# Second attention of a ViT block: scores as one float32 product, biases of q and k added on GpSimd, a PSUM bank written for each use, new step lists

## The reference, cut to what matters

```python
h = tok(x)                                   # (128, 197, 192)
h = h + attn(_layernorm(h), Wq, bq, ...)     # first attention, 12 heads of 16
# second attention, x = _layernorm(h)
qkv = (x @ qkv_w + qkv_b).reshape(B, N, 3, H, HD)
q, k, v = ...                                # HD = 64, H = 12
q = _layernorm(q, q_norm_w, q_norm_b)        # over the 64 of a head, times w, plus b
k = _layernorm(k, k_norm_w, k_norm_b)
attn = softmax(einsum('bhqd,bhkd->bhqk', q * scale, k))
o = einsum('bhqk,bhkd->bhqd', attn, v)
o = masked_gates[..., None] * o              # gates from softmax and top-2 of 10
h = h + (o.reshape(B, N, H * HD) @ proj_w + proj_b)
```

## Time and profile before

| | |
|---|---|
| median of 3 runs | 6208.34 us |
| time of the profiled execution | 6208.79 us |
| its span, first to last instruction | 6207.0 us |
| PE busy (share of the span) | 5808.5 us (94%) |
| PEld | 4640.1 us (75%) |
| DVE | 5098.7 us (82%) |
| ACT | 4936.7 us (80%) |
| POOL | 2435.5 us (39%) |
| transfers | 17 GB/s, 5.6% of the 16 DMA engines |
| granted clock of TensorE, mean | 0.993 |

### The profile page before, as it was taken

The page is one execution under the profiler, slowest core; times in us unless marked ns, Lnnn a source line. Parts: engine busy times, 40 slices in busy tenths (PEclk is TensorE's granted clock), DMA queues, the critical chain, the costliest instruction groups (busy, mean ns, idle before and its releaser), DMA issues.

```text
span 6207.0 us, 204792 instructions
## 1 busy us (share of the span) xinstructions
PE 5808.5 (94%) x63792; PEld 4640.1 (75%) x63792; DVE 5098.7 (82%) x16573; ACT 4936.7 (80%) x18945; POOL 2435.5 (39%) x2438
## 2 busy tenths in 40 slices
PE   3899999999999999999999999999999999999998
PEld 3677777777777777777777777777777777777776
DVE  4788888888888888888888888888888888888886
ACT  1788887887888888788888878888887887888886
POOL 0333443343344344334334433433433343444343
PEclk8999999999999999999999999999999999999999
DMA  1000000000000000000000000000000000000000
GB/s 64 16 19 16 15 19 16 15 15 19 16 15 19 16 15 15 19 16 15 19 16 15 17 17 16 15 19 16 15 19 16 15 15 19 16 15 19 16 15 5
DMA packets 60493, 106.58 MB, mean 17 GB/s; under 512 B 8077, under 2 KB 33945, under 8 KB 60129
## 3 DMA queue, kind: packets, MB, share of 16 engines
q1 hardware_dynamic: 60456, 106.12, 5.6%
HBM read 86.72 MB, written 19.37 MB: 17 GB/s over the span
## 4 chain that ended last, share of the span: by engine, by line
PE 60%; DVE 27%; issue 8%; ACT 4%; DVEq 1%; SPq 0%; ACTq 0%; POOL 0%; DMA 0%; POOLq 0%
PE bank L500 54%; PE bank L684 6%; DVE nmax L1034 5%; DVE qkn L1028 4%; DVE qk L916 3%; ACT p L745 3%; DVE kl L1018 2%; DVE ql L1012 2%; DVE v L996 2%; DVE nmax L921 2%; DVE gn L1044 1%; DVE x1T L911 1%; DVE rsum L1041 1%; DVE rsum L929 0%; DVE glog L963 0%
## 5 line engine op out<-in xcount | busy, mean ns | idle before, releaser
L489 POOL TENSOR_TENSOR pq<-pq,gn 99x788 f32<-99x788 f32 x768 | 1166.3, 1519 | 2302.6 <-DVE gn L1044 2302.4
L792 ACT ACTIVATE pq<-bank,nmax 99x197 f32<-99x197 f32 x3072 | 1303.1, 444 | 300.5 <-DVE nmax L1034 300.5
L745 ACT ACTIVATE p<-bank,nmax 99x197 f32<-99x197 f32 x3072 | 1281.9, 441 | 31.2 <-DVE nmax L921 15.1
L921 DVE TENSOR_REDUCE nmax<-bank 99x2 f32<-99x394 f32 x1536 | 824.4, 565 | 320.8 <-PE bank L500 316.8
L1034 DVE TENSOR_REDUCE nmax<-bank 99x2 f32<-99x394 f32 x1536 | 837.9, 559 | 125.3 <-PE bank L500 110.1
L798 ACT ACTIVATE pT<-bank 99x394 f32<-99x394 f32 x1536 | 773.1, 512 | 152.7 <-PE bank L684 152.3
L684 PE MATMUL bank<-ident,pq 99*99 99x99 f32 (+1 forms) x6144 | 784.7, 260 | 14.8 <-ACT pq L792 3.3
L500 PE MATMUL bank<-x2T,wqkc 128*128 128x198 f16 (+1 forms) x7680 | 796.3, 249 | 1.0 <-ACT qkc L756 0.6
L684 PEld LDWEIGHTS bank<-ident,pq 99*99 99x99 f32 (+1 forms) x6144 | 647.5, 166 | 171.1 <-issue 78.4
L500 PEld LDWEIGHTS bank<-x2T,wqkc 128*128 128x128 f16 (+1 forms) x7680 | 650.0, 98 | 99.1 <-ACT qkc L756 41.4
L792 ACT ACTIVATION_READ_ACCUMULATOR pq<-bank,nmax 99x1 f32 x3072 | 687.9, 224 | 0.0
(11 more groups left out here) (149 smaller groups left out, 11877.8 us busy)
## 6 DMA issues: line engine op xcount, KB each, us to landing
xa<-in_xa SPq DMA_DIRECT2D x128, 300.1 KB
xb<-in_xb SPq DMA_DIRECT2D x128, 300.1 KB
out_tokens<-res SPq DMA_DIRECT2D x128, 74.2 KB
out_tokens<-res SPq DMA_DIRECT2D x128, 73.5 KB
p<-in_wq SPq DMA_DIRECT2D x1, 1152.0 KB
pT<-in_wk SPq DMA_DIRECT2D x1, 1152.0 KB
qkc<-in_basis SPq DMA_DIRECT2D x1, 661.5 KB
sq<-in_wq SPq DMA_DIRECT2D x1, 576.0 KB
```

What stands on the lines that cost most here:

```text
L489: nc.gpsimd.tensor_tensor(pair, pair, factor, op=ALU.mult).then_inc(s_sc.up(), 1)
L745: last = nc.scalar.activation(p1[0:TC, h, c, :], psum("s1", h)[0:TC, c * T:c * T + T], ACT.Exp, bias=nmax1[:, c, h:h + 1], accum_out=sum1[ ...
L792: last = nc.scalar.activation(pq[0:TC, h % SLOTS, c, 0:T], psum("s2", h)[0:TC, c * T:c * T + T], ACT.Exp, bias=nmax2[:, h, c:c + 1], accum ...
L921: V.tensor_reduce(nmax1[:, :, h], psum("s1", h)[0:TC, 0:2 * T].rearrange("p (a b) -> p a b", a=2), op=ALU.max, axis=AX.X, negate=True).the ...
```

## The change

Tiles `qh`, `ql`, `kh`, `kl` and the steps that write them (ACT `rstd` and `kh`, DVE `lo` and `kl`) go. A new POOL step `bias` adds `ln_b` to both q and k of a pair in one instruction on 128 x 396 elements, from `qkn` into a new float32 tile `qkb`. Step `s2` waits for it (`s_qk`) and makes the scores by float32 matmuls straight from `qkb`: 4 a pair instead of 12, still on two halves of the array's rows and in two banks. DVE's `rstd` waits for the bias of three pairs earlier in place of `kl` and `lo` (the ring of `qkn`). Banks are no longer rings: each use in PE's list names its bank (`@15`: head n in bank 1, head n + 1 in bank 5). All four lists are new. Four more iterations are straight code instead of the loop (`LEAD`), two at each end. The helper `lasts`, which found the last reader of each bank, is replaced by a wait for the last head of a group, and bank `ms` is counted as number 0.

```diff
 
 
 
-BANKS = {"tok": (2,), "x1T": (2,), "qk1": (0, 1), "v1": (2,), "s1": (0, 1), "ctx": (2,), "wo": (2,),
-         "x2T": (6,), "gl": (6,), "qk": (6,), "v2": (6,), "ms": (7,),
-         "rstd": (3, 4, 5), "s2": (3, 4, 5), "pT": (3, 4, 5), "o2": (3, 4, 5), "proj": (3, 4, 5)}
-
 ORDER = {
     "pe": """
-3:tok 0:pT_9 0:pT_10 0:o2_3 0:pT_11 1:rstd1 0:o2_4 0:o2_5 1:s2_0 0:proj 1:v2_1 3:x1T 1:rstd2 1:s2_2 1:v2_2 1:rstd3
-3:qk1_0 1:v2_3 3:v1 3:s1_0 2:x2T 1:rstd4 1:s2_4 3:qk1_1 2:qk0 1:rstd5 1:pT_0 3:s1_2 2:gl 1:s2_6 1:pT_1 3:qk1_2 2:qk1
-1:pT_2 3:s1_4 3:ctx0 2:qk2 1:pT_3 1:s2_8 2:qk3 3:s1_6 2:ms0 2:qk4 1:o2_0 1:o2_1 3:s1_8 1:pT_4 1:pT_5 2:qk5 2:ms1
-3:s1_10 3:ctx1 1:s2_10 1:o2_2 2:ms2 2:v2_0 3:ctx2 1:pT_6 3:wo 1:pT_7 1:pT_8 2:rstd0
+3:tok@2 0:pT_8@0 0:pT_9@7 0:pT_10@4 0:pT_11@5 1:rstd2@3 0:o2_2@6 0:o2_3@1 0:o2_4@6 0:o2_5@4 1:s2_0@15 1:s2_2@64
+3:x1T@0 0:proj@2 3:qk1_0@5 1:v2_0@7 3:qk1_1@2 3:s1_0@04 3:s1_2@63 1:v2_1@5 1:v2_2@1 3:qk1_2@7 1:s2_4@50 1:rstd3@2
+1:pT_0@4 1:v2_3@1 2:x2T@3 1:pT_1@6 3:s1_4@57 1:s2_6@24 2:qk0@6 3:v1@3 2:qk1@0 1:rstd4@1 1:rstd5@2 2:qk2@6 3:s1_6@51
+3:s1_8@34 2:qk3@0 1:pT_2@6 2:gl@2 2:qk4@7 2:qk5@5 1:pT_3@2 1:s2_8@03 3:s1_10@75 1:pT_4@6 3:ctx0@1 1:o2_0@4 1:s2_10@72
+2:ms0@0 2:ms1 2:ms2 3:ctx1@5 3:ctx2@6 1:o2_1@3 1:pT_5@4 1:pT_6@5 3:wo@1 1:pT_7@7 2:rstd0@4 2:rstd1@3
 """,
     "dve": """
-3:fold 1:v2_0 1:var2 0:gr5 2:wo 1:rstd0 1:gate3 3:tok 1:kl0 1:rstd1 1:lo0 2:nx2 1:s2_0 3:nx1 1:lo1 1:s2_1 0:proj 1:kl1
-1:v2_1 1:rstd2 3:x1T 1:s2_2 1:lo2 1:v2_2 1:rstd3 1:s2_3 3:qk1_0 1:v2_3 1:kl2 3:s1_0 1:lo3 1:gr0 3:s1_1 2:x2T 1:s2_4
-1:s2_5 1:rstd4 1:gr1 1:kl3 3:qk1_1 1:rstd5 3:s1_2 3:s1_3 2:gl 1:s2_6 1:kl4 3:ctx0 1:lo4 1:s2_7 1:gr2 3:qk1_2 3:s1_4
-1:gr3 3:s1_5 1:lo5 1:s2_8 1:s2_9 3:s1_6 3:s1_7 1:kl5 3:ctx1 3:s1_8 3:s1_9 1:gr4 2:gate1 3:s1_10 3:s1_11 2:gate2
-1:s2_10 3:ctx2 1:s2_11
+0:gr4 3:fold 1:var2 0:gr5 1:rstd0 1:rstd1 2:wo 3:tok 1:gate1 3:nx1 1:s2_0 1:s2_1 1:s2_2 1:rstd2 2:nx2 3:x1T 1:s2_3
+1:gate2 0:proj 1:gate3 3:qk1_0 1:gr0 1:v2_0 3:s1_0 3:s1_1 3:s1_2 3:qk1_1 1:v2_1 3:s1_3 1:gr1 1:v2_2 1:s2_4 1:rstd3
+3:qk1_2 1:v2_3 1:s2_5 2:x2T 3:s1_4 1:s2_6 1:gr2 3:s1_5 1:s2_7 1:rstd4 1:rstd5 3:s1_6 3:s1_7 1:gr3 3:s1_8 2:gl 3:ctx0
+3:s1_9 1:s2_8 3:s1_10 3:s1_11 1:s2_9 3:ctx1 1:s2_10 3:ctx2 1:s2_11
 """,
     "act": """
-3:x1T 1:rstd2 1:kh2 1:s2_2 3:qk1_0 1:rstd3 1:kh3 1:s2_3 3:v1 2:x2T 3:s1_0 3:s1_1 1:s2_4 3:qk1_1 1:s2_5 2:qk0 1:kh4
-1:pT_0 3:s1_2 3:s1_3 1:rstd4 1:s2_6 3:qk1_2 2:qk1 1:pT_1 1:s2_7 1:rstd5 3:s1_4 1:pT_2 2:qk2 1:pT_3 3:s1_5 1:kh5 2:qk3
-1:s2_8 3:s1_6 3:s1_7 1:s2_9 1:o2_0 2:qk4 3:s1_8 2:gate0 3:s1_9 1:o2_1 3:ctx0 1:pT_4 2:qk5 1:pT_5 3:s1_10 3:s1_11
-3:ctx1 1:s2_10 2:var0 3:ctx2 2:var1 1:s2_11 1:pT_6 1:o2_2 1:pT_7 2:rstd0 1:pT_8 2:kh0 1:pT_9 1:pT_10 1:o2_3 1:pT_11
-1:o2_4 1:o2_5 2:kh1 2:rstd1 2:s2_0 2:s2_1
+3:x1T 1:s2_1 1:s2_2 1:s2_3 3:qk1_0 3:qk1_1 3:s1_0 3:s1_1 3:s1_2 3:qk1_2 3:s1_3 1:s2_4 1:pT_0 2:x2T 1:pT_1 1:s2_5
+3:s1_4 2:qk0 1:s2_6 1:s2_7 3:v1 2:qk1 3:s1_5 2:qk2 3:s1_6 3:s1_7 2:qk3 3:s1_8 2:qk4 2:qk5 1:pT_2 3:s1_9 1:pT_3 3:s1_10
+1:s2_8 3:s1_11 1:pT_4 1:s2_9 1:o2_0 2:var0 3:ctx0 3:ctx1 3:ctx2 2:var1 1:s2_10 1:o2_1 1:pT_5 1:s2_11 1:pT_6 1:pT_7
+1:pT_8 1:pT_9 2:gate0 1:pT_10 1:o2_2 1:pT_11 1:o2_3 1:o2_4 1:o2_5 2:s2_0
 """,
     "pool": """
-3:root1 1:h2c 2:h2b 1:sc0 1:sc1 1:sc2 2:sq0 3:h1b 2:sq1 2:sq2 1:sc3 2:sq3 1:sc4 2:sq4 2:sq5 1:sc5 3:root2
+3:root1 1:sc0 1:bias2 1:sc1 1:bias3 3:h1b 1:sc2 1:h2c 2:sq0 1:bias4 2:sq1 1:bias5 2:sq2 2:h2b 2:sq3 2:sq4 2:sq5 1:sc3
+1:sc4 1:sc5 2:bias0 3:root2 2:bias1
 """,
 }
 
@@ -165,27 +161,23 @@
 def steps_of(engine):
 
     for entry in ORDER[engine].split():
-        ahead, step = entry.split(":")
+        ahead, step = entry.split("@")[0].split(":")
         name = step if step in WHOLE else step.split("_")[0] if "_" in step else step.rstrip("0123456789")
         number = step[len(name):].lstrip("_")
         yield int(ahead), name, int(number) if number else 0
 
 
 DEPTH = max(ahead for engine in ORDER for ahead, _, _ in steps_of(engine))
+LEAD = 2
 
 
 def bank_uses():
 
-    uses, in_bank, turn = {}, [[] for _ in range(8)], {}
-    for ahead, name, n in steps_of("pe"):
-        if name not in BANKS or (name == "ms" and n < 2):
-            continue
-        for i in (n, n + 1) if name in ("s1", "s2") else (n,):
-            ring = BANKS[name]
-            b = ring[turn.get(ring, 0) % len(ring)]
-            turn[ring] = turn.get(ring, 0) + 1
-            uses[name, i] = (b, ahead, len(in_bank[b]))
-            in_bank[b].append(ahead)
+    uses, in_bank = {}, [[] for _ in range(8)]
+    for entry, (ahead, name, n) in zip(ORDER["pe"].split(), steps_of("pe")):
+        for i, b in enumerate(entry.partition("@")[2]):
+            uses[name, n + i] = (int(b), ahead, len(in_bank[int(b)]))
+            in_bank[int(b)].append(ahead)
     return uses, in_bank
 
 
@@ -298,10 +290,7 @@
         rootsq = sb("rootsq", [128, TP])
         rs_mask = sb("rs_mask", [128, TP], F16)
         rs_hl = sb("rs_hl", [128, TP], F16)
-        qh = sb("qh", [128, 6, TP], F16)
-        ql = sb("ql", [128, 6, TP], F16)
-        kh = sb("kh", [128, 6, TP], F16)
-        kl = sb("kl", [128, 6, TP], F16)
+        qkb = sb("qkb", [128, 6, 2, TP])
         nmax2 = sb("nmax2", [TC, H, 2])
...
             shifts = [other - ahead + (p < place) for p, other in enumerate(in_bank[b])]
             if isinstance(img, int):
                 return sum(min(max(img + shift, 0), images) for shift in shifts)
-            return img * len(shifts) + sum(shifts)
+            whole = sum(shifts) // len(shifts)
+            return (img + whole) * len(shifts) + sum(shifts) - whole * len(shifts)
 
         def room_for(img, *key):
...
@@ -404,11 +386,11 @@
                     if not edge or 0 <= i + ahead < images:
                         steps[name](i + ahead, n)
 
-            for i in range(-DEPTH, 1):
+            for i in range(-DEPTH, LEAD + 1):
                 go(i, True)
-            with eng.Fori(1, images - DEPTH) as i:
+            with eng.Fori(LEAD + 1, images - DEPTH - LEAD) as i:
                 go(i, False)
-            for i in range(images - DEPTH, images):
+            for i in range(images - DEPTH - LEAD, images):
                 go(i, True)
 
         @block.sync
@@ -492,7 +474,12 @@
                 pool.wait_ge(*read_out(img, "qk", t))
                 nc.gpsimd.tensor_tensor(sq[:, t], qkc[:, t], qkc[:, t], op=ALU.mult).then_inc(s_sq.up(), 1)
 
-            run_phases(pool, "pool", {"sq": square, "root1": root1, "root2": root2, "h1b": h1b_, "h2b": h2b_, "h2c": h2c_, "sc": scale})
+            def bias(img, t):
+
+                pool.wait_ge(*read_out(img, "rstd", t))
+                nc.gpsimd.tensor_tensor(qkb[:, t], qkn[:, t % QKN_SLOTS], ln_b[:].unsqueeze(2).to_broadcast([128, 2, TP]), op=ALU.add).then_inc(s_qk.up(), 1)
+
+            run_phases(pool, "pool", {"bias": bias, "sq": square, "root1": root1, "root2": root2, "h1b": h1b_, "h2b": h2b_, "h2c": h2c_, "sc": scale})
 
         @block.tensor
         def _(pe):
...
@@ -662,16 +648,13 @@
                 assert uses["s2", h][0] != uses["s2", h + 1][0]
                 for i in heads:
                     pe.wait_ge(*room_for(img, "s2", i))
-                pe.wait_ge(*s_lo.at(img, t + 1))
-                pe.wait_ge(*s_kl.at(img, t + 1))
-                for c in range(2):
-                    cols = slice(c * TC, c * TC + TC)
-                    for n, (q, k) in enumerate(((qh, kh), (ql, kh), (qh, kl))):
-                        for i in heads:
-                            r = slice(64 * (i % 2), 64 * (i % 2) + 64)
-                            last = mm(psum("s2", i)[0:TC, c * T:c * T + T], q[r, t, cols], k[r, t, 0:T], n == 0, n == 2)
-                            if c == 1 and n == 2:
-                                last.then_inc(full("s2", i), 1)
+                pe.wait_ge(*s_qk.at(img, t + 1))
+                for c in range(2):
+                    for i in heads:
+                        r = slice(64 * (i % 2), 64 * (i % 2) + 64)
+                        last = mm(psum("s2", i)[0:TC, c * T:c * T + T], qkb[r, t, 0, c * TC:c * TC + TC], qkb[r, t, 1, 0:T])
+                        if c == 1:
+                            last.then_inc(full("s2", i), 1)
 
             def pT_(img, h):
 
...
+                    nc.scalar.activation(lnvar[:], psum("ms", 0)[:, 0:TP], ACT.Ln, bias=eps[:, 0:1]).then_inc(s_root.up(), 1)
                     act.wait_ge(*s_root.at(img, 1))
                     nc.scalar.activation(root[:], lnvar[:], ACT.Exp, scale=-0.5).then_inc(s_root.up(), 1)
                 if n == 1:
                     act.wait_ge(*s_root.at(img, 2))
                     nc.scalar.activation(rootsq[:], root[:], ACT.Square).then_inc(s_root.up(), 1)
 
-            def rstd_(img, t):
-
-                act.wait_ge(*read_out(img, "rstd", t))
-                nc.scalar.activation(qh[:, t, :], qkn[:, t % QKN_SLOTS, 0, :], ACT.Identity, bias=ln_b[:, 0:1]).then_inc(s_hi.up(), 1)
-
-            def k_high(img, t):
-
```

(21 more changed lines are left out.)

36 lines of the change are left out of this document (13 added, 23 removed).

## The result

The changed kernel takes 5675.02 us (median of 4 runs, 5672.85 to 5678.02 us), beside 6207.98 us for the kernel before (4 runs, 6203.64 to 6211.28 us): 0.9142 of its time, 95% interval 0.9126 to 0.9158. The forecast was 5936 us with a range from 5840 to 6170 us. The direction was right, the size was not: 533 us came off where 272 were forecast.

The account below looks back on a forecast made before the run. Two thirds of a period were taken as bound by PE's work, one third by DVE's list; 44.4 + 1.0 - 1.05 + 0.6 gives 45.0 us an image, 2.13 less over 128 images: 5936 us, range 5840 to 6170.

Parts of the forecast that it names:

- PE's own work, old order, without hidden waits: PE's work per image in the kernel before, all waiting taken out: about 44.4 us, may be 44.2 to 44.9.
- new scores: PE's s2 with four float32 products: 0.82 us a pair for 0.65, +1.0 us an image, bounds +0.2 and +5.2.
- waits left: PE's waiting per image after the change: 0.6 us in place of 2.7, with 0 and 2.7 as ends.
- seven more joins: Equal steps made neighbours in PE's new list, 0.15 us saved each: -1.05 us an image, bounds 0 and -1.4.
- Which wait is next: PE's next waits after the change: s2_6 for bias3 through POOL, and s1_0 for DVE's low parts.
- rival 3: POOL's six new instructions each hold DVE's two-input ones 0.41 us, 2.5 us an image: 6256 us; chance 0.03.
- The walk through the new list: Hand count from PE's rstd1 to the x1T copy: DVE some 12 us, PE 13, so DVE is a microsecond ahead.
- Rival 1: Row halves don't work together in float32 in s2: 1.51 us a pair for 0.82, 6384 us, slower; chance 0.13.
- Rival 4: The float32 product isn't full precision, a pair takes one round of half length: some 5680 us; chance 0.01.
- The bias: POOL's new addition on 128 x 396 float32: 0.87 us each, 5.2 us an image, price 0 on the path.
- Hidden waits: Late starts in PE's old slots hidden behind the tail of the matmul ahead: 0.5 us an image, an estimate.
- DVE and ACT busy: Busy time per image without the high and low parts: DVE 39.45 to 34.4 us, ACT 38.5 to 32.9 us.

Follow-up runs that it names:

- relief alone: The kernel before without the steps that write qh, ql, kh and kl, three products still made, old order: 6106.76 us, 0.9845.
- the order alone: The changed kernel's lists and named banks, but the old three-product scores with qh, kh, ql, kl put back: 6710.95 us, 1.0806 of before.
- the serial form: The changed kernel with both heads' scores of a pair made on rows 0 to 63, so one after another: 6234.82 us, 1.005.
- short maximum: The changed kernel with DVE's row maximum reading 24 of 197 keys in each chunk: 5758.23 us, 0.928.
- ACT's work back: The changed kernel with ACT's twelve high parts made again and read by nobody: 6125.82 us, 0.9874.
- DVE's work back: The changed kernel with twelve DVE instructions like the low parts put in and read by nobody: 6590.92 us, 1.0617.

## Why the prediction was right or wrong

| per image, us | forecast | measured |
|---|---|---|
| PE's own work, old order, without hidden waits | 44.4 | 44.47 (relief alone) |
| new scores | +1.0 | +1.13 of own work in the old order (+0.94 in total), s2 slots 3.95 to 4.92 |
| joins and order | -1.05 | about -2.8 |
| PE's own work after | 44.35 | 42.84 |
| waits left | 0.6 | 0.26 |
| period | 45.0 | 43.10 |

- **The step that failed is the term "seven more joins" at 0.15 us each.** It stood for 1.05 us where the order gave 2.5 to 2.9, so it accounts for 1.5 to 1.8 us of the 1.9 by which the period was missed, some 200 of the 261 us. The price of one kind of join was taken from `o2` and put on all. Two joined `s1` are a different thing: 0.50 us for both in one place and 0.66 in the other, against 0.47 for one alone. The four heads of two such steps have their own 32 rows each, and the rows show them working together. The three joined `ms` take 1.02 us for 24 products, where they took 1.48 us before in separate slots. With all slots of an image added up, without the listed waits, the kinds that the seven joins touch take 1.91 us less than in the old order with the new scores (`s1` 0.91, `ms` 0.49, `s2` 0.23, `ctx` 0.17, `o2` 0.11); the other 0.96 us, half of it in the transposes, were not counted at all. What should have been counted is the change of the tile's shape: 14 fewer, not seven, about 1.7 us at 0.08 to 0.17 each, and with the 0.4 to 0.5 us that the `s1` pairs gain by working together some 2.2 us (an estimate from these slots). The remaining half microsecond or so is open; waits hidden in the old order's transposes, as above, may be part of it. The lower bound of that term, -1.4 us, was no bound: no row of another kind of step stood behind it.
- **The waits** were right in kind (DVE's list would no longer bind) and somewhat too high, 0.6 for 0.26 us. "Which wait is next" was wrong: not `s2_6` for bias3 but `pT` behind DVE's `glog`, by way of rival 3's mechanism.
- **Relief and order.** I took DVE's relief to be what makes its list reach PE in time. The runs show that the relief alone leaves the waits (19.1 and 17.6 us over twenty images and more, as before) and the order alone makes new ones of 1.7 us and more. The walk through the new list was the right argument, since it took both together.
- **The scores** were right: 0.85 us for 0.82 from `o2` on column halves. Rival 1 is refuted by the serial form. Rival 4's time, some 5680 us, is nearly the measured one, and that is chance: its mechanism, a pair in half the time, is refuted by the same 0.85 us.
- **The bias** was right: 0.845 us for 0.87. **Hidden waits** of 0.5 us in the old slots were right too: 44.98 - 44.47.
- **DVE and ACT busy** came out at 37.3 and 33.8 us, not 34.4 and 32.9. `gn` (421 for 231 ns, six an image) and the first `vs` (487 for 222 ns, three an image) are 1.9 us of DVE's 2.9: time in which DVE is held, not work.
- **Rival 3** as priced, 0.41 us a meeting and all on the path, didn't come. Its mechanism did, with 1.73 us at one place that costs PE 0.26. The Trainium skill (SBUF — State Buffer, SBUF: two separate sides) states the lock for the whole instruction; here a waiting DVE instruction stood through several of POOL's, which the rows above show and the rule as put doesn't say. Nor is the absence of a gap the whole condition: in the kernel before, POOL's `h1b` followed the square just as closely (at 3127.98), and the product of the earlier trace rows ended at 3128.04, with the square.
- **The range** ended at 5840 us because its low end was a period of 44.2 us, little less than the forecast's own work with no waits at all (44.35); no case stood for a larger gain of the order.

## What to carry to other kernels

Price the neighbours of a step on TensorE, not only the step: the same instructions took 45.6 us in one order and 42.8 us in another. Count how often the shape of the stationary tile changes along PE's list, not how often the kind of step does, and price each from start-to-start slots; steps on different rows of the array can nearly vanish when they are neighbours. A term that stands on one row needs an honest lower bound. In a kernel whose engines are this close, making one engine earlier can cost time, so look at which of DVE's two-input instructions would begin beside a run of POOL's, and who waits behind it.

## What the runs showed of the hardware

- **A DVE instruction with two SBUF inputs can be held through several POOL instructions** that follow each other without a gap, squares and biases on 128 x 396: 1.73 us (changed kernel), 2.49 us (short maximum), 3.33 us (`gr3` moved, two products), 3.64 us (longer bias), for work that takes 0.16 to 0.4 us. What lets it in is open: the case of the earlier trace rows was let in after one square.
- **A stall of PE can cost twice.** In the kernel with the longer bias PE was busy for 2.02 of 4.00 us, and then worked for 8 us at a mean granted clock of 0.57, near the lower of the two levels of 1.2 and 2.4 GHz (0.50), before it was back at 1.00:

```profile
3009.00:3013.00 4.00, 2.02 (x26) 1.78 (x24) 3.97 (x7) 1.43 (x7) 4.00 (x6) 1.00 0.00 0
3013.00:3021.00 8.00, 7.81 (x56) 4.84 (x56) 3.65 (x13) 6.94 (x30) 3.55 (x4) 0.57 0.00 0
3021.00:3029.00 8.00, 8.00 (x104) 6.79 (x101) 5.92 (x18) 4.97 (x18) 3.90 (x3) 1.00 0.23 77
```

  There 56 matmuls start in 8 us, and 104 in the next 8. With ACT's work back, a wait of 1.35 us (up to 3016.59) has the same sequel, 8 us at 0.57. Not every such wait has it: with DVE's work back the clock falls to 0.57 after a wait of 2.18 us and stays at 1.00 after one of 1.45 us (at 3032.34). This is why the mean clock of these kernels is 0.94 to 0.95, and why they came out slower than their waits alone would make them; the new lists with the old scores ran at 0.93 too.
- **Float32 products work side by side on two halves of the array's rows**: 0.85 us for a pair against 1.50 one after another. **Two neighbouring steps on four groups of 32 rows** take 0.50 us together (0.66 at the other place), one alone 0.47.
- **A change of the stationary tile's shape costs PE 0.08 to 0.17 us, a change of the kind of product none**: `ms` 0.33 us before `ctx` (both 128 x 32), 0.47 before a full tile; a transpose 0.35 us before `v2`, 0.48 before `s1`.
